# A two-layer decoder on one core: GpSimd takes over the last splits, xr_apply and an earlier rstd, and the small work of the last attention stands at other heads

## The chip, the cores and the metric

The kernel runs on one core of a Trainium2 chip. The metric is the device time of one execution in microseconds (us); lower is better. Three runs of the kernel before gave 401.40, 405.24 and 403.68 us, median 403.68. One further execution was profiled: 400.37 us.

## What is computed

Eight sequences (B = 8) of 256 positions (S = 256) with 128 features (D = 128) go through six residual steps. All attention inputs come from a layer norm.

```python
x = x + _L0_attn_ref(_layernorm(x), ...)               # 16 heads, head size 8
x = x + _L0_xattn_ref(_layernorm(x), ctx_1024, ...)    # one head of 128, CROSS
x = x + _L0_ffn_ref(_layernorm(x), ...)                # routed, 2 x 256 rows
x = x + _L1_attn_ref(_layernorm(x), ...)               # one head, causal, CAUSAL
x = x + _L1_xattn_ref(_layernorm(x), ctx_1024, ctx_1024, ...)  # 16 heads, LAST
x = x + _L1_ffn_ref(_layernorm(x), ...)                # light FFN for all rows,
# heavy FFN for the 128 rows of each sequence that a coordinate descent selects

att = softmax(einsum('bhqd,bhkd->bhqk', q, k) / sqrt(head size))
out = einsum('bhqk,bhkd->bhqd', att, v)
```

The heavy rows of the last step are chosen by scores s = x . routing_token, followed by 50 steps of coordinate descent over the 256 positions and a top-128.

## The kernel before

Each of the five engines runs a program that is written out by hand: the order of the work on an engine is the order of the calls in its function, and engines wait for each other on semaphores. An engine takes its instructions strictly in order, so what stands behind a waiting instruction waits too.

The span has four stages. The first attention (16 heads) lies at about 10 to 125 us; the middle, with items of CROSS, CAUSAL and the first few of LAST and the routed FFN, to about 228 us; the last attention (16 heads, keys and values from the context) to 347 us; then the tail with ranks, coordinate descent and the two FFNs. The work items are numbered in `WORK`: 0 to 7 the first attention, 8 to 26 the middle, 27 to 31 the rest of LAST. The eight LAST items are 18, 22, 26, 27, 28, 29, 30, 31; as steps of a 16-head attention they are also counted m = 8 to 15 (`item(m)` and `many(n)` translate), and the sequences are taken in this order as b = 0 to 7.

The last attention runs iterations i = 8 to 15, each over heads h = 0 to 15. Iteration i does, on TensorE, the scores of m = i again (with the maximum subtracted, s_ps, L1321) and the first scores of m = i + 1 (L1330), whose maximum per row VectorE takes (`row_max`, L938, from PSUM); ScalarE makes the exponentials (L643), and TensorE sums the values (`weighted_sum`, L1367) once in four heads. Around these stand the small steps of other items:

- For the item three steps ahead, x: `ln_stats` (VectorE, L911 and L914), `rstd_step_` (GpSimd, L503 and L505), `ln_apply` (VectorE, L922), `xn_transpose` (TensorE, L1269), `xnT_copy` (ScalarE), `qk_project` (L1277, L1281), `qk_copy` (ScalarE, L665, writes qkf), and `split`. `split` takes the fp32 queries and keys in qkf apart into three bf16 terms with four instructions (L399, L401, L402, L404). The sync queue (SP) then writes the terms into the stack that the score matmuls read, in twelve transfers (L462). `v_project` and `v_copy` make the values at h = 14 and 15.
- For i - 1: `normalise` (VectorE), `o_transpose` and `out_project` (TensorE, L1398), `residual` (VectorE, L957).
- For i - 2: `z_norm_stats` and `z_route` (VectorE, L1023 to L1037: moments of the row, and its product with the routing vector), `z_norms` (GpSimd, L551 to L566), `xr_apply` (VectorE, L1045: centred and scaled rows for the last FFN), `xr_transpose` (TensorE, L1392).

prep_ps, one place in PSUM, serves several of TensorE's small steps in turn: `prep_free` holds what the next one has to wait for. qkf has two slots, an item n uses n % 2, so that `qk_copy(n)` waits for the readers of item n - 2. Splits of m = 8, 9 and 10 are on VectorE (at items 18 and 22 of the middle and at h = 6 of iteration 8), those of m = 11 to 15 on GpSimd. GpSimd's program for these is the loop

```python
elif 2 <= n < B or n >= B + AHEAD_C:
    rstd_step_(item(n))
add_bias(n)
if lo == B and n >= lo + 5:
    z_norms(n - lo - 5)
if lo == B and n == lo + 5:
    heavy_bias_parts()
if n not in FIRST:
    split(pool, n)
```

`add_bias` (L513) and `value_bias` (L519) add a bias to x ahead of its residual; `heavy_bias_parts` is seven small instructions of the last FFN, needed in the tail. `f_norm_stats`, `f_rstd_step`, `f_apply` (L1007) are the layer norm of the routed FFN; `softmax_bias` (L966 to L979) is VectorE's part of a CAUSAL item. The functions that the change touches and those that call them:

## Time and profile before

| | us | share of the span |
|---|---|---|
| median of three runs | 403.68 | |
| profiled execution | 400.37 | |
| its span | 398.6 | |
| TensorE matmuls (PE) | 355.0 | 89% |
| TensorE weight loads (PEld) | 210.8 | 53% |
| VectorE (DVE) | 324.3 | 81% |
| ScalarE (ACT) | 265.1 | 67% |
| GpSimd (POOL) | 140.8 | 35% |

The mean granted TensorE clock of this execution was 0.983 of full speed. Weight loads overlap matmuls. A line of the page such as "L938 DVE TENSOR_REDUCE negmax_sb<-s_ps 128x2 bf16<-128x512 f32 x256" is a group of 256 instructions of line 938 of the kernel, with output and input and their shapes. A bracket behind a row, as [1.20 <-DVE negmax_sb L938], is time in which the engine stood idle before it, and the instruction that released it. A row with x2 or more joins neighbouring instructions of a line, and its time is from the first start to the last end. The chain of work that ended last consists of 55% TensorE, 22% VectorE, 6% ScalarE, 5% GpSimd and 3% transfers.

### The profile page before, as it was taken

The page shows a single profiled execution, that of the slowest core. Times are in us where ns is not written, and L with a number is a line of the kernel's source. Part 1 is how long each engine was busy: PE and PEld are TensorE (multiplying, and loading weights), DVE is VectorE, ACT ScalarE, POOL GpSimd, SP SyncE. Part 2 cuts the span into 40 slices and gives each one's busy share as a digit, 9 for nine tenths or more (in the row PEclk, how much of TensorE's full clock was granted, in tenths as well). Part 3 has the DMA queues.
Part 4 walks back from the last instruction along what each step waited for, and adds up shares of the span by engine and source line. Part 5 has one row for each costly group of instructions (what it writes and reads, how often), then busy time and mean ns, then how long its engine had stood idle before and what let it go on. Part 6 is the DMA issues. An engine that isn't in the chain of part 4 may idle for free.

```text
span 398.6 us, 9595 instructions
## 1 busy us (share of the span) xinstructions
PE 355.0 (89%) x3246; PEld 210.8 (53%) x3246; DVE 324.3 (81%) x898; ACT 265.1 (67%) x594; POOL 140.8 (35%) x243
## 2 busy tenths in 40 slices
PE   6999999999999889977797867999889899989994
PEld 5775454545444478866286633444344344447664
DVE  6778989998996377895569585899999997579995
ACT  3446888888878567755507755778767787765751
POOL 8633754475100033342004323447555221280001
PEclk9999999999999999996999997899999999999999
DMA  7442332223420000002000203220321200000003
GB/s 221 126 106 67 82 103 75 72 51 102 130 86 2 2 0 3 0 16 66 0 2 21 62 2 102 59 62 22 82 61 28 75 2 4 2 0 2 0 2 105
DMA packets 35829, 19.99 MB, mean 50 GB/s; under 512 B 4150, under 2 KB 34790, under 8 KB 35782
## 3 DMA queue, kind: packets, MB, share of 16 engines
q1 hardware_dynamic: 34982, 17.81, 16.8%
q10 hardware_dynamic: 608, 1.18, 0.8%
q8 instruction: 27, 0.44, 0.5%
q0 software_dynamic: 192, 0.39, 0.4%
q14 instruction: 20, 0.16, 0.1%
HBM read 5.58 MB, written 1.05 MB: 17 GB/s over the span
## 4 chain that ended last, share of the span: by engine, by line
PE 55%; DVE 22%; issue 7%; ACT 6%; POOL 5%; DMA 3%; SPq 2%; ACTq 0%; POOLq 0%; DVEq 0%
PE pv_ps L1367 11%; PE s_ps L1321 10%; DVE negmax_sb L938 8%; PE s_ps L1424 4%; PE out_ps L1479 3%; PE s_ps L1447 3%; PE s_ps L1655 3%; PE s_ps L1330 3%; PE prep_ps L1277 2%; ACT probT_sb L643 2%; PE s_ps L1507 2%; DVE xn_sb L922 2%; SPq L462 2%; PE out_ps L1398 2%; PE prep_ps L1281 2%
## 5 line engine op out<-in xcount | busy, mean ns | idle before, releaser
L938 DVE TENSOR_REDUCE negmax_sb<-s_ps 128x2 bf16<-128x512 f32 x256 | 163.3, 688 | 25.1 <-PE s_ps L1330 24.8
L643 ACT ACTIVATE probT_sb<-s_ps 128x512 f32<-128x512 f32 x256 | 142.3, 596 | 35.0 <-PE s_ps L1321 32.5
L1321 PE MATMUL s_ps<-stack_sb 63*128 63x256 bf16 x512 | 90.2, 275 | 11.2 <-DVE negmax_sb L938 3.7
L1330 PE MATMUL s_ps<-stack_sb 62*128 62x256 bf16 x512 | 87.3, 275 | 1.9 <-DVE negmax_sb L938 1.4
L1367 PE MATMUL pv_ps<-probT_sb,v_aug_sb 128*32 128x256 f32 x1024 | 69.9, 391 | 0.5 <-ACT probT_sb L643 0.5
L1321 PEld LDWEIGHTS s_ps<-stack_sb 63*128 63x128 bf16 x512 | 31.0, 94 | 68.5 <-ACT probT_sb L643 41.9
L503 POOL TENSOR_SCALAR rstd_sb<-mv_sb 128x2 f32<-128x2 f32 x32 | 7.1, 222 | 118.0 <-DVE mv_sb L914 117.9
L1367 PEld LDWEIGHTS pv_ps<-probT_sb,v_aug_sb 128*32 128x32 f32 x1024 | 27.0, 110 | 25.8 <-issue 13.2
L1330 PEld LDWEIGHTS s_ps<-stack_sb 62*128 62x128 bf16 x512 | 29.6, 94 | 7.3 <-DVE negmax_sb L938 3.2
L665 ACT ACTIVATE qkf_sb<-prep_ps,b_qkv_sb 128x256 f32<-128x256 f32 x56 | 23.9, 470 | 11.9 <-PE prep_ps L1281 10.3
L1189 DVE SCALAR_TENSOR_TENSOR late_sb<-late_sb,level_sb,k_inv_sb 8x256 f32<-8x256 f32 x49 | 23.2, 474 | 1.8
L505 POOL TENSOR_TENSOR rstd_sb<-rstd_sb,minus_half_sb 128x2 f32<-128x2 f32 x32 | 23.1, 722 | 2.7
L922 DVE TENSOR_SCALAR xn_sb<-x_all_sb,mv_sb,rstd_sb 128x128 f32<-128x128 f32 x64 | 20.4, 384 | 3.1 <-POOL rstd_sb L505 2.8
L1277 PE MATMUL prep_ps<-xnT_sb,w_att_sb 128*128 128x256 f32 x64 | 21.5, 418 | 0.3
L1424 PE MATMUL s_ps<-xrT_sb,d_w_sb 128*128 128x512 f32 x40 | 19.5, 611 | 0.8 <-ACT late_sb L730 0.8
L399 POOL CAST parts_sb<-qkf_sb 128x512 bf16<-128x512 f32 x11 | 6.7, 610 | 31.4 <-ACT qkf_sb L665 26.8
L730 ACT ACTIVATE late_sb<-s_ps,d_b_sb 128x512 f32<-128x512 f32 x20 | 13.4, 686 | 6.1 <-PE s_ps L1424 6.1
L513 POOL TENSOR_TENSOR x_all_sb<-x_all_sb,b_vo_sb 128x256 f32<-128x256 f32 x16 | 12.3, 775 | 14.1 <-DVE xn_sb L922 14.1
L991 DVE SCALAR_TENSOR_TENSOR x_all_sb<-out_ps,den_inv_sb,x_all_sb 128x128 f32<-128x128 f32 x32 | 9.7, 346 | 8.4 <-PE out_ps L1479 8.2
L745 ACT ACTIVATE prob_sb<-s_ps,negbias_sb 128x256 f32<-128x256 f32 (+1 forms) x32 | 14.0, 447 | 3.0 <-DVE negbias_sb L979 3.0
L911 DVE BATCH_NORM_STATS2 stats_sb<-x_all_sb 128x6 f32<-128x128 f32 x64 | 15.2, 280 | 0.5 <-DMA x_all_sb<-x 0.3
L1655 PE MATMUL s_ps<-d_w_sb,late_sb 128*128 128x128 f32 x128 | 15.6, 275 | 0.0
(207 smaller groups left out, 647.2 us busy)
## 6 DMA issues: line engine op xcount, KB each, us to landing
stack_sb<-parts_sb SPq DMA_DIRECT2D x186, 64.0 KB, 2.1
x_all_sb<-x SPq DMA_DIRECT2D x4, 256.0 KB, 3.0
ctxT_sb<-ctxT ACTq DMA_DIRECT2D x2, 512.0 KB, 6.3
f_w_sb<-f_w SPq DMA_DIRECT2D x2, 512.0 KB, 3.7
out<-x_all_sb SPq DMA_DIRECT2D x4, 256.0 KB, 2.4
d_w_sb<-d_w SPq DMA_DIRECT2D x2, 320.0 KB, 3.6
w_att_sb<-w_att SPq DMA_DIRECT2D x2, 256.0 KB, 4.0
stack_sb<-maxrow_sb ACTq DMA_DIRECT2D x32, 4.0 KB
```

The source lines that it names most:

```text
L505: pool.tensor_tensor(rstd[:, u, :], rstd[:, u, :], minus_half[:, 0:NT], ALU.pow).then_inc(rstd_ready, 1)
L643: act.activation(probT[:, c % 8], s2_ps[c % 2][:, :, :], ACT.Exp, scale=DH ** -0.5).then_inc(exp_ready, 1)
L665: act.activation(qkf[:, n % 2, a, :], prep_ps[:, a, :], ACT.Identity, bias=b_qkv[:, layer(n), a:a + 1]).then_inc(qk_ready, 2 if layer(n) = ...
L922: i = dve.tensor_scalar(xn[:, u, k, :], x_all[:, tiles(n).start + k, :], mv[:, u, k, 0:1], rstd[:, u, k:k + 1], ALU.subtract, ALU.mult)
L938: dve.tensor_reduce(negmax[:, n % 2, :, max_column(max_head(h))], first_bank(c)[:, :, :], axis=AX.X, op=ALU.max, negate=True).then_inc(max ...
L1189: dve.scalar_tensor_tensor(out=min_junk[:, :], in0=e_row[:, :], scalar=level[:, a:a + 1], in1=k_inv[:, :], op0=ALU.min, op1=ALU.mult, accu ...
L1277: i = pe.matmul(prep_ps[:, 0, :], w_att[:, l, 0, :], xnT[:, u, :], start=True, stop=True)
L1321: i = pe.matmul(s2_ps[c % 2][:, k, :], stack[rows, s3, 1, h // 2, k * P:(k + 1) * P], stack[rows, s3, 0, h // 2, :], start=True, stop=True)
L1330: i = pe.matmul(first_bank(c)[:, k, :], stack[rows, s3, 0, hp, k * P:(k + 1) * P], stack[rows, s3, 1, hp, :], start=True, stop=True)
L1367: i = pe.matmul(pv_ps[0][32 * j:32 * j + 32, g // 2, :], v_cols[:, k, first:first + 32], probT[:, h % 8, k, :], start=(g % 2 == 0 and k == ...
L1424: pe.matmul(up_bank(c), d_w1[:, f, :], xrT[:, 2 * S * q:2 * S * (q + 1)], start=True, stop=True).then_inc(d_h_psum, 1)
L1655: i = pe.matmul(heavy_bank(b)[:, k, :], d_hT[:, q % 2, f, toks[k]], d_w2[:, f, :], start=False, stop=(f == NC - 2 and k == NT - 1))
```

## The change

Three parts. (1) qkf gets a third slot, which the LAST items of the middle (18, 22, 26) use; `before(n)` gives the last item in the same slot, for which `qk_copy(n)` waits. (2) The splits of m = 8, 9 and 10 go from VectorE to GpSimd's loop over the middle, `xr_apply` goes from VectorE to GpSimd for all sequences, and in the last attention GpSimd makes `rstd` one item earlier; `heavy_bias_parts` goes behind the split. (3) In the last attention the small steps stand at other heads: on VectorE ln_stats at h = 11 of the iteration before (was 1), ln_apply 3 (was 2), normalise 5 (4), residual 13 (15), z_norm_stats 1 (3), z_route 8 (7); on ScalarE xnT_copy 5 (3), qk_copy 8 (7), oT_copy 10 (11); on TensorE xn_transpose 5, behind the weighted sum (4, ahead of it), qk_project 8 (7), o_transpose 10 (11), out_project 12 (15).

```diff
-        qkf = sb("qkf", [P, 2, 2, S])
+        qkf = sb("qkf", [P, 3, 2, S])
+        def slot(n):
+            return 2 if WORK[n][0] == LAST and n < MID_END else n % 2
+        def before(n):
+            return max((j for j in range(n) if slot(j) == slot(n)), default=None)
         def split(eng, m):
-            n, u, w = m, m % 2, item(m) % 2
+            n, u, w = m, m % 2, slot(item(m))
-            def xr_late(b):
+            def xr_apply(b):
                 pool.wait_ge(rn_ready, b + 1)
-                pool.wait_ge(xrT_psum, b - 1)
+                if b >= 2:
+                    pool.wait_ge(xrT_psum, b - 1)
                         if layer(n - 2) == CAUSAL:
                             value_bias(n - 2)
+                        if layer(n - 3) == LAST:
+                            split(pool, many(n - 3))
                     value_bias(LAST_ITEM)
+                    split(pool, B + 2)
-                    elif 2 <= n < B or n >= B + AHEAD_C:
+                    elif 2 <= n < B or n == B + AHEAD_C:
                         rstd_step_(item(n))
                     add_bias(n)
                     if lo == B and n >= lo + 5:
                         z_norms(n - lo - 5)
+                    if lo == B and lo + AHEAD_C <= n < lo + B - 1:
+                        rstd_step_(item(n + 1))
+                    if lo == B and n >= lo + 5:
+                        xr_apply(n - lo - 5)
+                    if n not in FIRST:
+                        split(pool, n)
                     if lo == B and n == lo + 5:
                         heavy_bias_parts()
-                    if n not in FIRST:
-                        split(pool, n)
             for b in range(3, B):
                 z_norms(b)
-                if b >= B - 2:
-                    xr_late(b)
+                xr_apply(b)
...
-                if n >= 2:
-                    if IS_MID[n - 2]:
-                        act.wait_ge(sc_psum, mid(n - 2) + 1)
+                j = before(n)
+                if j is not None:
+                    if IS_MID[j]:
+                        act.wait_ge(sc_psum, mid(j) + 1)
...
-                        if layer(i) == LAST and i != MID_END - 1:
-                            split(dve, many(i))
...
+                        if lo == B and h == 11 and prepared(i + 1, lo):
+                            ln_stats(prepared(i + 1, lo))
-                        if h == at(lo, 0, 1) and ln is not None and ln != 1:
+                        if (lo == 0 and h == 0 or (i, h) == (B, 1)) and ln is not None and ln != 1:
-                        if (i, h) == (B, 6):
-                            split(dve, B + 2)
-                        if h == 2 and ln is not None and ln != 1:
+                        if h == at(lo, 2, 3) and ln is not None and ln != 1:
-                        if h == 4 and has(i - 1, lo):
+                        if h == at(lo, 4, 5) and has(i - 1, lo):
-                        if h == 15 and has(i - 1, lo):
+                        if h == at(lo, 15, 13) and has(i - 1, lo):
-                            if h == 3:
+                            if h == 1:
                                 z_norm_stats(i - 2 - B)
-                            if h == 7:
+                            if h == 8:
                                 z_route(i - 2 - B)
-                            if h == 12:
-                                xr_apply(i - 2 - B)
...
+                        if lo == B and h == 5 and x is not None:
+                            if prep_free:
+                                pe.wait_ge(*prep_free)
+                            xn_transpose(x)
+                            prep_free = (xnT_ready, x + 1)
-                        if h == 7 and x is not None:
+                        if h == at(lo, 7, 8) and x is not None:
                             qk_project(x)
-                        if h == 11 and has(i - 1, lo):
+                        if h == at(lo, 11, 10) and has(i - 1, lo):
                             o_transpose(i - 1)
-                        if h == 15 and has(i - 1, lo):
+                        if h == at(lo, 15, 12) and has(i - 1, lo):
                             out_project(i - 1)
```

What the change does to the order of the instructions is shown at three places. The first is GpSimd around the start of the last attention. In the kernel before, value_bias (L519) is followed by three add_bias (L513), rstd of item 27 (L503, L505), the add_bias of m = 11 and the split of m = 11:

```order
L519 TENSOR_TENSOR x_all_sb<-x_all_sb,b_vo_sb 128x256 x2
L513 TENSOR_TENSOR x_all_sb<-x_all_sb,b_vo_sb 128x256 x3
L503 TENSOR_SCALAR rstd_sb<-mv_sb 128x2
L505 TENSOR_TENSOR rstd_sb<-rstd_sb,minus_half_sb 128x2
L513 TENSOR_TENSOR x_all_sb<-x_all_sb,b_vo_sb 128x256
L399 CAST parts_sb<-qkf_sb 128x2x256
```

In the changed kernel lines have shifted by 8: value_bias is L527, split L407 to L412, add_bias L521, rstd L511 and L513:

```order
L527 TENSOR_TENSOR x_all_sb<-x_all_sb,b_vo_sb 128x256 x2
L407 CAST parts_sb<-qkf_sb 128x2x256
L409 TENSOR_TENSOR rest_sb<-qkf_sb,parts_sb 128x512
L410 TENSOR_TENSOR parts_sb<-qkf_sb,parts_sb 128x2x256
L412 TENSOR_TENSOR parts_sb<-rest_sb,parts_sb 128x2x256
L521 TENSOR_TENSOR x_all_sb<-x_all_sb,b_vo_sb 128x256 x3
L511 TENSOR_SCALAR rstd_sb<-mv_sb 128x2
L513 TENSOR_TENSOR rstd_sb<-rstd_sb,minus_half_sb 128x2
L521 TENSOR_TENSOR x_all_sb<-x_all_sb,b_vo_sb 128x256
L511 TENSOR_SCALAR rstd_sb<-mv_sb 128x2
L513 TENSOR_TENSOR rstd_sb<-rstd_sb,minus_half_sb 128x2
L407 CAST parts_sb<-qkf_sb 128x2x256
```

The split of m = 10 has come in between value_bias and the add_bias, ahead of rstd(27), and rstd(28) now stands ahead of the split of m = 11. The second place is GpSimd in the middle, around the routed FFN's rstd (L593 and L595, later L602 and L604). Before:

```order
L593 TENSOR_SCALAR f_rstd_sb<-f_mv_sb 128x4
L595 TENSOR_TENSOR f_rstd_sb<-f_rstd_sb,minus_half_sb 128x4
L519 TENSOR_TENSOR x_all_sb<-x_all_sb,b_vo_sb 128x256
L503 TENSOR_SCALAR rstd_sb<-mv_sb 128x2
L505 TENSOR_TENSOR rstd_sb<-rstd_sb,minus_half_sb 128x2
```

and in the changed kernel:

```order
L602 TENSOR_SCALAR f_rstd_sb<-f_mv_sb 128x4
L604 TENSOR_TENSOR f_rstd_sb<-f_rstd_sb,minus_half_sb 128x4
L527 TENSOR_TENSOR x_all_sb<-x_all_sb,b_vo_sb 128x256
L407 CAST parts_sb<-qkf_sb 128x2x256
L409 TENSOR_TENSOR rest_sb<-qkf_sb,parts_sb 128x512
L410 TENSOR_TENSOR parts_sb<-qkf_sb,parts_sb 128x2x256
L412 TENSOR_TENSOR parts_sb<-rest_sb,parts_sb 128x2x256
L511 TENSOR_SCALAR rstd_sb<-mv_sb 128x2
```

Here the split of m = 8 has come in behind value_bias(19) and ahead of rstd(22). The third place is GpSimd in iteration 10, where z_norms(0) ends with xr_scale. Before, heavy_bias_parts (prob_sb, the first three of its seven rows) follows, and then the split of m = 13:

```order
L562 TENSOR_SCALAR rnorm_sb<-rnorm_sb 128x2
L564 TENSOR_TENSOR rnorm_sb<-rnorm_sb,minus_half_sb 128x2
L566 TENSOR_TENSOR xr_scale_sb<-rnorm_sb,z_rstd_sb 128x2
L573 MEMSET prob_sb 128x128
L574 MEMSET prob_sb 128x128
L575 CAST prob_sb<-d_b_sb 3x128
```

and in the changed kernel:

```order
L574 TENSOR_TENSOR xr_scale_sb<-rnorm_sb,z_rstd_sb 128x2
L511 TENSOR_SCALAR rstd_sb<-mv_sb 128x2
L513 TENSOR_TENSOR rstd_sb<-rstd_sb,minus_half_sb 128x2
L596 TENSOR_SCALAR xr_sb<-x_all_sb,z_mv_sb,xr_scale_sb 128x128 x2
L407 CAST parts_sb<-qkf_sb 128x2x256
L409 TENSOR_TENSOR rest_sb<-qkf_sb,parts_sb 128x512
L410 TENSOR_TENSOR parts_sb<-qkf_sb,parts_sb 128x2x256
L412 TENSOR_TENSOR parts_sb<-rest_sb,parts_sb 128x2x256
L581 MEMSET prob_sb 128x128
```

Between z_norms and the split there is now rstd of the next item and xr_apply, and heavy_bias_parts has gone behind the split.

## Rows read from the trace of the kernel before

**Rows 1.** Windows, iterations 8 to 13: length, PE, PEld, DVE, ACT, POOL, clock.

```profile
228.06:247.42 19.36, 13.14 (x132) 6.25 (x132) 14.21 (x29) 10.91 (x22) 5.69 (x7) 0.91 0.18 45
247.42:261.86 14.44, 14.44 (x152) 7.04 (x153) 11.98 (x24) 10.96 (x24) 5.72 (x7) 0.88 0.21 52
261.86:276.37 14.51, 13.63 (x156) 6.67 (x156) 14.36 (x37) 11.56 (x26) 7.87 (x21) 1.00 0.23 58
276.37:291.45 15.08, 13.66 (x155) 6.58 (x156) 13.94 (x33) 11.40 (x25) 10.26 (x18) 1.00 0.22 54
291.45:306.74 15.29, 13.81 (x155) 6.59 (x155) 15.17 (x36) 11.51 (x25) 8.30 (x16) 1.00 0.21 54
306.74:319.48 12.74, 11.50 (x145) 5.32 (x145) 12.67 (x31) 10.11 (x21) 2.98 (x9) 1.00 0.25 64
```

**Rows 2.** Waits of 262 to 333 us: engine, line, releaser: total, times, longest.

```profile
PE prep_ps L1269 <- DVE xn_sb L922: 2.2, 3, 0.9
...
PE s_ps L1321 <- DVE negmax_sb L938: 2.1, 5, 0.8
```

**Rows 3.** Instructions of xr_apply: on VectorE in two stretches, on GpSimd.

```profile
L1045 DVE TENSOR_SCALAR xr_sb<-x_all_sb,z_mv_sb,xr_scale_sb x4: 1121/1162/1202, 288.4 to 304.7; 128x128 f32<-128x128 f32 x4
...
L1045 DVE TENSOR_SCALAR xr_sb<-x_all_sb,z_mv_sb,xr_scale_sb x6: 333/336/342, 317.7 to 344.4; 128x128 f32<-128x128 f32 x6
...
L587 POOL TENSOR_SCALAR xr_sb<-x_all_sb,z_mv_sb,xr_scale_sb x4: 792/798/811, 351.9 to 357.9; 128x128 f32<-128x128 f32 x4
```

**Rows 4.** Timeline of VectorE, then of GpSimd, iteration 11.

```profile
288.39 2.25 DVE L1045 TENSOR_SCALAR xr_sb<-x_all_sb,z_mv_sb,xr_scale_sb 128x128 f32<-128x128 f32 x2
...
287.60 0.61 POOL L399 CAST parts_sb<-qkf_sb 128x512 bf16<-128x512 f32 x1
288.29 1.16 POOL L401 TENSOR_TENSOR rest_sb<-qkf_sb,parts_sb 128x512 f32<-128x512 f32 x1
...
290.64 1.16 POOL L404 TENSOR_TENSOR parts_sb<-rest_sb,parts_sb 128x512 bf16<-128x512 f32 x1
```

**Rows 5.** Timeline of TensorE at the end of iteration 11.

```profile
290.05 0.71 PE L1398 MATMUL out_ps<-w_att_sb,oT_sb 128*128 128x128 f32 x4
291.08 0.44 PE L1392 MATMUL prep_ps<-ident_sb,xr_sb 128*128 128x128 f32 x2 [0.32 <-ACT v_aug_sb L699]
```

**Rows 6.** Iteration 8: chain of waits, timelines of TensorE, ScalarE, GpSimd.

```profile
235.57 0.43 DVE parts_sb L399
...
238.07 0.53 SPq L462
...
245.11 2.06 DMA stack_sb<-parts_sb
...
238.92 0.27 PE L1321 MATMUL s_ps<-stack_sb 63*128 63x256 bf16 x1 [1.20 <-DVE negmax_sb L938]
...
247.42 0.27 PE L1321 MATMUL s_ps<-stack_sb 63*128 63x256 bf16 x1 [2.49 <-DMA stack_sb<-parts_sb]
...
225.83 0.84 ACT L665 ACTIVATE qkf_sb<-prep_ps,b_qkv_sb 128x256 f32<-128x256 f32 x2 [0.67 <-PE prep_ps L1281]
...
231.34 0.71 POOL L505 TENSOR_TENSOR rstd_sb<-rstd_sb,minus_half_sb 128x2 f32<-128x2 f32 x1
232.83 0.72 POOL L513 TENSOR_TENSOR x_all_sb<-x_all_sb,b_vo_sb 128x256 f32<-128x256 f32 x1 [0.78 <-DVE xn_sb L922]
```

**Rows 7.** Busy time by window, iteration 9; last columns clock, DMA, GB/s.

```profile
248.20:251.60 3.40, 3.40 (x29) 1.57 (x22) 2.76 (x10) 2.48 (x6) 0.95 (x2) 0.51 0.39 101
```

**Rows 8.** Middle, item 18: timelines of GpSimd, VectorE, TensorE.

```profile
175.38 1.05 POOL L519 TENSOR_TENSOR x_all_sb<-x_all_sb,b_vo_sb 128x256 f32<-128x256 f32 x1
...
178.48 1.08 DVE L1007 TENSOR_SCALAR f_xn_sb<-x_all_sb,f_mv_sb,f_rstd_sb 128x128 f32<-128x128 f32 x4
...
180.81 0.60 DVE L922 TENSOR_SCALAR xn_sb<-x_all_sb,mv_sb,rstd_sb 128x128 f32<-128x128 f32 x2
...
181.56 0.66 PE L1269 MATMUL pv_ps<-ident_sb,xn_sb 128*128 128x128 f32 x2 [4.37 <-DVE xn_sb L922]
```

20 lines of the change are left out of this document (6 added, 14 removed).

## Prediction

> **What bounds the kernel now.** I read the page first: TensorE is busy 89% of the span, VectorE 81%, ScalarE 67% and GpSimd 35%. TensorE comes first, but the share is a mean over stages, so I cut the last attention at the first score matmul of each iteration (the table of windows, [rows 1]). Iteration 8 takes 19.36 us and TensorE works 13.14 of them. Iteration 9 takes 14.44, all of it TensorE, at a granted clock of 0.88. Iterations 10, 11 and 12 take 14.51, 15.08 and 15.29, with 13.6 to 13.8 us of TensorE and 14.36, 13.94 and 15.17 of VectorE. In 13, and 14 is like it, VectorE is busy 12.67 of 12.74 us: there VectorE is the bound. The table of waits says what TensorE stands for in 10 to 14: xn (2.2 us) and the row maxima (2.1 us), both VectorE's [rows 2]. So work taken from VectorE pays in iteration 8 and in 10 to 14, and only down to TensorE's own work, 13.6 to 13.8 us and its small gaps in 10 to 12.
>
> **What goes from VectorE in 10 to 14: xr_apply.** Its row is the key to the change. Alone, one of its two instructions takes 336 ns; in iterations 11 and 12 it takes 1121 to 1202 [rows 3]. The timelines say why: at 288.39 VectorE starts the pair and needs 2.25 us, while GpSimd's split has a 1.16 us operation at 288.29, a second behind it, and its last at 290.64 [rows 4]. The pair ends as the second does: each of the two waited for one GpSimd instruction. On GpSimd xr_apply takes 2 x 0.80 us [rows 3].
> The Trainium skill (SBUF — State Buffer, "Who interferes with whom") says that a VectorE tensor_scalar in a two-port mode and a GpSimd instruction take a shared pair of ports for a whole instruction each, and that tensor_reduce never contends; this trace agrees (1162 ns against 336). Were the ports shared by halves, the pair would have taken some 1.2 us, and its removal 1 us less in 11 and 12.
>
> VectorE so gets back some 0.5 us (the pair overlapped, alone) in 10, 13 and 14 and 2.2 in 11 and 12. Most of TensorE's wait for xn goes too: ln_stats moves to h=11 of the iteration before, and xn_transpose stands a head later, behind a weighted_sum. Against this, out_project (0.71 us at 290.05) now stands at h=12. At h=15 it filled time in which TensorE waits for v_copy anyway; 0.32 us of that wait are left before xr_transpose [rows 5], and it grows by what out_project covered. So I do not take TensorE's 13.7 us as the new period of 10, 11 and 12 but 14.0: -0.5, -1.1 and -1.3. For 13 and 14 I take -0.6 and -0.4, for 15, which has little of this, -0.1. **Sum of 10 to 15: -4.0.**
>
> **Iteration 8.** The chain of waits [rows 6] runs from VectorE's split(10) (235.57 to 238.06) through the sync queue's twelve issues (238.07 to 245.11) to the last transfer's 2.06 us and TensorE's wait of 2.49 us at 247.42: 9.1 us from the split's end. TensorE also waited 1.20 us at 238.92 (and twice 0.20 behind it) for row maxima queued behind the split. The first excerpt shows split(10) on GpSimd ahead of the last attention. What it needs is qk_copy(26), at 225.83 and over by 226.7, in the new third slot. At 0.61 and three times 1.16, 4.2 with its gaps [rows 4], it ends near 231.0, its transfers land near 240.1, and both waits, 4.1 us, go. But rstd(27) then stands behind the split and three add_bias of 0.72: 231.0 + 2.2 + 0.95 = 234.1, against 232.05 now. ln_apply(27) follows, xn_transpose comes at about 234.85, and TensorE stands up to 1.8 us there, partly in place of 0.8 that it stood before. It would reach iteration 9 between 243.0 and 244.7, the second if half the clock is granted again near its end, as the iteration's mean of 0.91 shows it now. I take 243.9: **-3.5** (-2.7 to -4.4).
>
> **Iteration 9.** From 248.2 to 251.6 the granted clock is 0.51, the 1.2 GHz level, with TensorE busy throughout [rows 7]; just before, it had stood for 2.49 us. Half the speed for 3.4 us is 1.7 us lost. Without the standing most of it should go: **-1.5** (0 to -1.7). The price is read; that the standing is its cause, one trace can't show.
>
> **The middle, item 18.** VectorE's split(8) goes to GpSimd, which can start it only behind value_bias(19) (175.38, 0.7 us without company) and ends it near 180.4 (second excerpt). In that time VectorE, earlier than now by a split of some 2.5 us, comes to f_apply's four tensor_scalars, of xr_apply's kind, which alone take 1.08 us together [rows 8]. If each waits for one GpSimd operation, as xr_apply's did, they run after 176.1, 176.8, 177.9 and 179.1, and the small product behind them near 180.3. Then come softmax_bias, 1.3, and ln_apply(21) near 181.6, against 180.8: +0.8. The other end is no collision: 2.5 us early. TensorE waits for exactly this xn, 4.37 us up to 181.56 [rows 8]. I take the nearer row, the collision: **+0.8** (-2.5 to +0.9). At item 22 VectorE's split is followed by a wait for TensorE: 0.
>
> **Sum.** -4.0 - 3.5 - 1.5 + 0.8 = -8.2 us. The profiled execution took 400.37 us (span 398.6 and 1.8 around it), so 392.2 is what I expect of its like. It lies 3.3 below the median of the runs, 403.68; against that I say 395.5. The tail's three further xr_apply, 3 x 1.6 us, fall to an engine that idles there: 0; if they were on the path, +1. One per cent, 4 us, is about what a measurement of this kernel can tell from no change.
>
> **Rivals.**
> A. *TensorE keeps most of it (within 1%).* Iteration 9 is all TensorE already, and 10 to 12 stand only 0.9 to 1.5 us above its busy time. If out_project at h=12 and the moved transposes put their 0.7 us on the path and the half clock comes anyway, 10 to 12 give 0.8 and not 2.9, iteration 9 nothing, iteration 8 its lower end 2.7, 13 to 15 their 1.1; less 0.8 in the middle that is 3.8: **399.9**. For it speaks iteration 9; against it TensorE's waits for VectorE in 10 to 14.
>
> B. *GpSimd becomes the bound (slower).* Its order in 11 is z_norms, rstd, xr_apply, split (third excerpt). Now the split starts 11.2 us into iteration 11 (287.60 less 276.37); rstd and xr_apply ahead of it add 2.55, z_route a head later some 0.3, and the split is 4.2: it ends 18.3 in, or 4.3 into iteration 12. With 9.1 to the last landing that is 13.4 of 14.0 us. split(15), without an rstd, ends some 3 us into 13: 12.1 of 12.1, no margin. Each microsecond by which GpSimd comes later beyond about 0.3 costs one in 11, 12 and 13. The gain is gone from 3 us on (3 x 2.7 = 8.1); at 4.5 us it is 3 x 4.2 - 8.2 = +4.4, **408**. For it speaks that GpSimd's busy time rises from 7.9 to 10.3 us by 1.6 in each of 10 to 12; against it, that this still leaves over 2 us of 14 and that what it waits for comes earlier.
> The Trainium skill (GPSIMD Engine Reference, "Performance versus the Vector engine") has GpSimd at 1.96 times VectorE's time for elementwise work and VectorE as the rule. The rows say more, 0.80 to 0.34 for xr_apply. By the rule the moves should lose; they do only in rival B.
>
> C. *The middle gains as well (faster).* f_apply slips in before GpSimd's split, ln_apply(21) comes 2.5 us early, and TensorE's shorter wait spares a half clock behind it as in iteration 9, 1.7 us: -8.2 - 0.8 - 2.5 - 1.7 = -13.2, **390.5**. For it speaks the length of that wait; against it, that value_bias holds f_apply until 176.1 already.
>
> **Chances.** The forecast has 0.50, with a range of its own of 392.5 to 398.5; C 0.16; A 0.24; B 0.10. So faster by over 1% is 0.66, within 1% 0.24, slower 0.10. The range, 390 to 401, leaves out B and the far halves of A and C.
>
> **What would show it.** Right are: an iteration 9 that begins without a wait for a transfer and at full clock; iterations 10 to 12 near 14.0 us with VectorE below 13, and 13 and 14 near 12.1; GpSimd's rstd(27) 2 us late in iteration 8; f_apply's four at about 1.1 us each. Rival A is seen as TensorE busy for the whole of 10 to 12 at 14.5; rival B as waits of TensorE for stack transfers or xr at the ends of 11 to 13. I am wrong in kind if half clock shows in more places than now, or if VectorE is still full in 11 and 12.

## The result, and the profile after

The changed kernel takes 399.93 us (median of 20 runs, 398.02 to 403.75) where the kernel before takes 404.35 (20 runs, 401.40 to 406.21). The ratio is 0.992, 95% interval 0.990 to 0.994: it is faster by 0.8%, some 3.3 us (the two medians alone are 4.4 apart), and not by the 8.2 us of the forecast. The ratios in this document are not quotients of medians, and executions over 1.5% above the fastest of the same kernel are left out of them. A second measurement of both, beside the experiments, gave 0.993 (0.989 to 0.996). By the bound of 1% this is the outcome "within 1%", and the 399.9 us lie where rival A had put them, though only in part for rival A's reasons, as will be seen. The profiled execution of the changed kernel took 402.32 us, over its own median, where that of the kernel before, 400.37, lay 4 us under its own. So the two pages differ the wrong way round, and the readings below go by stages.

The page of the changed kernel: the span, the busy times, and the chain by engine.

```profile
span 400.5 us, 9589 instructions
...
PE 355.7 (89%) x3246; PEld 212.1 (53%) x3246; DVE 314.8 (79%) x874; ACT 266.9 (67%) x594; POOL 160.4 (40%) x267
...
PE 69%; DVE 9%; ACT 8%; issue 6%; POOL 5%; DMA 1%; ACTq 0%; POOLq 0%; DVEq 0%
```

VectorE has lost 9.5 us and GpSimd gained 19.6. The chain that ended last was 55% TensorE and 22% VectorE; it is 69% and 9% now. VectorE has indeed been taken off the path. Below are the windows of iterations 8 to 14, with the columns of [rows 1]; here and from now on each iteration is cut at its first exponential on ScalarE. Lines have moved: L1324 and L1333 are the scores, L1395 is xr_transpose, L1023 f_apply, L954 row_max.

```profile
232.75:249.93 17.18, 13.22 (x132) 6.04 (x134) 12.45 (x30) 10.61 (x23) 9.16 (x14) 0.90 0.19 47
249.93:264.00 14.07, 13.09 (x154) 6.53 (x153) 12.17 (x26) 11.46 (x25) 6.14 (x8) 1.00 0.23 59
264.00:279.04 15.04, 13.57 (x158) 6.75 (x156) 13.20 (x33) 11.57 (x25) 9.24 (x18) 1.00 0.22 55
279.04:293.98 14.94, 13.47 (x158) 6.65 (x154) 13.53 (x33) 11.75 (x25) 11.58 (x25) 1.00 0.22 55
293.98:308.92 14.94, 13.47 (x158) 6.65 (x154) 12.81 (x29) 11.75 (x25) 10.08 (x17) 1.00 0.22 55
308.92:321.19 12.27, 11.36 (x148) 5.22 (x144) 11.98 (x27) 10.21 (x21) 5.32 (x11) 1.00 0.27 66
321.19:333.45 12.26, 11.37 (x144) 5.22 (x140) 11.98 (x29) 10.22 (x21) 4.24 (x10) 1.00 0.01 3
```

Against [rows 1]: iteration 8 is 2.2 us shorter, 9 is 0.4 shorter at full clock, 10 is 0.5 longer, 11 and 12 are 0.1 and 0.3 shorter. VectorE has 1.4 to 2.1 us to spare in 10 to 12, TensorE's busy time is as before, and it idles 1.5 us in each. 13 and 14 are 0.5 and 0.1 shorter. Iteration 15 took 14.73 us before and takes 15.61 now.

The table has the lengths of the stages in two profiles of each kernel (the second ones are from the experiments). "Middle" runs from the first exponential of iteration 7, in the first attention, to that of iteration 8. Each star marks 3.4 us at half clock.

| stage | before | before, second | after | after, second | forecast of the difference |
|---|---|---|---|---|---|
| middle | 104.50 ** | 103.76 * | 106.89 *** | 106.85 *** | +0.8 |
| iteration 8 | 19.33 * | 20.52 * | 17.18 * | 17.17 * | -3.5 |
| 9 | 14.46 * | 15.23 ** | 14.07 | 14.07 | -1.5 |
| 10, 11, 12 | 44.87 | 44.93 | 44.92 | 44.92 | -2.9 |
| 13, 14 | 25.13 | 25.15 | 24.53 | 24.50 | -1.0 |
| 15 | 14.73 | 14.73 | 15.61 | 15.63 | -0.1 |

(In the second profile of the kernel before, the 6.8 us counted to iteration 9 begin 1.7 us ahead of it. Iteration 15 ends with its last exponential.) The terms that missed by the most are 10 to 12, by 2.9 us, the middle, by 1.6 and 2.3, and 15, by 1.0. For 10 to 12 and 15 the forecast had -3.0 together, and the measured sum is +0.9. The rows of the table add up to +0.2 us in the first pair of profiles and -1.2 in the second, where the spans differ by +1.9 and +0.4. The rest, 1.9 and 1.7 us, lies ahead of the middle, where the change leaves the order as it was. In the second pair the changed kernel has 3.4 us at half clock there, from 21.0 us; in the first neither kernel has, and the cause is open.

### The profile page after: what moved, and what is told of

Same layout as the page of the kernel before. It is cut to its first block, busy times and chain, and to the rows that moved or that the text cites. A ratio compares the mean times of both kernels' runs of the same rounds, so it can differ in the third digit from the quotient of the medians.

```text
span 400.5 us, 9589 instructions
## 1 busy us (share of the span) xinstructions
PE 355.7 (89%) x3246; PEld 212.1 (53%) x3246; DVE 314.8 (79%) x874; ACT 266.9 (67%) x594; POOL 160.4 (40%) x267
## 4 chain that ended last, share of the span: by engine, by line
PE 69%; DVE 9%; ACT 8%; issue 6%; POOL 5%; DMA 1%; ACTq 0%; POOLq 0%; DVEq 0%
PE pv_ps L1370 15%; PE s_ps L1324 14%; PE s_ps L1427 4%; PE prep_ps L1280 3%; PE s_ps L1450 3%; ACT probT_sb L658 3%; PE s_ps L1333 3%; PE out_ps L1482 3%; PE s_ps L1663 3%; PE prep_ps L1284 2%; PE out_ps L1401 2%; PE s_ps L1510 2%; DVE negmax_sb L954 2%; PE s_ps L1467 2%; PE prep_ps L1307 2%
## 5 line engine op out<-in xcount | busy, mean ns | idle before, releaser
L954 DVE TENSOR_REDUCE negmax_sb<-s_ps 128x2 bf16<-128x512 f32 x256 | 163.9, 690 | 30.9 <-PE s_ps L1333 30.5
L658 ACT ACTIVATE probT_sb<-s_ps 128x512 f32<-128x512 f32 x256 | 144.3, 595 | 32.6 <-PE s_ps L1324 28.3
L1324 PE MATMUL s_ps<-stack_sb 63*128 63x256 bf16 x512 | 89.4, 273 | 9.2 <-ACT probT_sb L658 5.1
L1333 PE MATMUL s_ps<-stack_sb 62*128 62x256 bf16 x512 | 85.9, 274 | 3.8 <-DMA stack_sb<-parts_sb 2.4
L1324 PEld LDWEIGHTS s_ps<-stack_sb 63*128 63x128 bf16 x512 | 31.1, 94 | 64.4 <-ACT probT_sb L658 34.0
L511 POOL TENSOR_SCALAR rstd_sb<-mv_sb 128x2 f32<-128x2 f32 x32 | 7.1, 223 | 106.1 <-DVE mv_sb L930 105.9
L1333 PEld LDWEIGHTS s_ps<-stack_sb 62*128 62x128 bf16 x512 | 29.8, 94 | 9.2 <-DVE negmax_sb L954 3.2
L938 DVE TENSOR_SCALAR xn_sb<-x_all_sb,mv_sb,rstd_sb 128x128 f32<-128x128 f32 x64 | 22.4, 441 | 3.9 <-POOL rstd_sb L513 3.6
L513 POOL TENSOR_TENSOR rstd_sb<-rstd_sb,minus_half_sb 128x2 f32<-128x2 f32 x32 | 22.9, 714 | 2.7
L407 POOL CAST parts_sb<-qkf_sb 128x512 bf16<-128x512 f32 x14 | 8.5, 609 | 28.9 <-ACT qkf_sb L681 28.9
L521 POOL TENSOR_TENSOR x_all_sb<-x_all_sb,b_vo_sb 128x256 f32<-128x256 f32 x16 | 11.5, 726 | 16.0 <-DVE xn_sb L938 15.9
L412 POOL TENSOR_TENSOR parts_sb<-rest_sb,parts_sb 128x512 bf16<-128x512 f32 x14 | 16.2, 1158 | 1.1
L409 POOL TENSOR_TENSOR rest_sb<-qkf_sb,parts_sb 128x512 f32<-128x512 f32 x14 | 16.2, 1156 | 1.1
```

The source lines that it names most:

```text
L409: eng.tensor_tensor(rest[:, :, :], qkf[:, w], parts[:, u, :, 0, :], ALU.subtract).then_inc(rest_ready, 1)
L513: pool.tensor_tensor(rstd[:, u, :], rstd[:, u, :], minus_half[:, 0:NT], ALU.pow).then_inc(rstd_ready, 1)
L658: act.activation(probT[:, c % 8], s2_ps[c % 2][:, :, :], ACT.Exp, scale=DH ** -0.5).then_inc(exp_ready, 1)
L938: i = dve.tensor_scalar(xn[:, u, k, :], x_all[:, tiles(n).start + k, :], mv[:, u, k, 0:1], rstd[:, u, k:k + 1], ALU.subtract, ALU.mult)
L954: dve.tensor_reduce(negmax[:, n % 2, :, max_column(max_head(h))], first_bank(c)[:, :, :], axis=AX.X, op=ALU.max, negate=True).then_inc(max ...
L1324: i = pe.matmul(s2_ps[c % 2][:, k, :], stack[rows, s3, 1, h // 2, k * P:(k + 1) * P], stack[rows, s3, 0, h // 2, :], start=True, stop=True)
```

## The experiments

All times are compared with runs of the kernel before on the same chip. "Middle" and the iterations are cut as above.

### 1. GpSimd's moves alone, and the heads alone

e1_moves keeps the splits of m = 8, 9 and 10 and xr_apply on GpSimd and puts all the rest back:

```diff
-                        if lo == B and h == 11 and prepared(i + 1, lo):
-                            ln_stats(prepared(i + 1, lo))
-                        if (lo == 0 and h == 0 or (i, h) == (B, 1)) and ...
+                        if h == at(lo, 0, 1) and ln is not None and ln != 1:
-                    if lo == B and lo + AHEAD_C <= n < lo + B - 1:
-                        rstd_step_(item(n + 1))
...
-                        if h == at(lo, 15, 12) and has(i - 1, lo):
+                        if h == 15 and has(i - 1, lo):
                             out_project(i - 1)
```

> The changed kernel with the small steps of the last attention at the heads of the kernel before, and rstd not one item earlier: what is left is GpSimd's splits of m = 8, 9, 10 and xr_apply. Theory H (the moved heads took the saving back: in the changed kernel TensorE waits 0.96 us for v_copy at the end of each of iterations 10 to 12, where out_project stood, and 0.5 us behind the moved xn_transpose): iterations 10 to 12 fall from 14.95 to 14.2-14.5 us, iteration 8 stays at 17.2, and the time is 397 to 398.5 us, ratio to before 0.983 to 0.987. Rival M (the moves to GpSimd gain only what iteration 8 shows, the heads are neutral or help): iterations 10 to 12 at 14.9 or more, time 400 or more, ratio 0.990 or above.

Measured: 404.87 us, ratio 1.002 (0.999 to 1.005): no gain. Yet iterations 9, 10 and 12 are 13.35, 14.52 and 14.52 us, up to 0.7 shorter than in the changed kernel. What eats the gain stands in its windows of iterations 10 and 11,

```profile
266.36:280.88 14.52, 13.62 (x158) 6.67 (x154) 13.34 (x34) 11.23 (x24) 8.32 (x16) 1.00 0.22 57
280.88:298.99 18.11, 15.01 (x158) 7.13 (x154) 13.61 (x33) 11.40 (x26) 12.57 (x26) 0.91 0.18 45
```

and in its timeline of GpSimd in iteration 11,

```profile
284.26 0.41 POOL L589 TENSOR_TENSOR prob_sb<-prob_sb 3x128 bf16<-3x128 f32 x1
...
285.08 0.73 POOL L513 TENSOR_TENSOR rstd_sb<-rstd_sb,minus_half_sb 128x2 f32<-128x2 f32 x1
```

and of TensorE:

```profile
286.59 0.41 PE L1268 MATMUL prep_ps<-ident_sb,xn_sb 128*128 128x128 f32 x2 [2.78 <-DVE xn_sb L936]
```

rstd waits on GpSimd until split and the last part of heavy_bias_parts (L589) are through, xn is 2.78 us late, and half clock follows (3.4 us from 287.1): 3.6 us in one iteration. In iteration 8 the same wait is 2.81 us long and 6.8 us at half clock begin in it. This is the mechanism of rival B, in the two places where rstd is queued behind a split. Theory H had the time wrong (397 to 398.5 us) and was right about the iterations that have no such wait. Rival M's "400 or more" holds, but not its 14.9 us or more for them.

e2_heads is the other half: everything on VectorE as before, the small steps at the heads of the change, rstd one item earlier.

```diff
-        qkf = sb("qkf", [P, 3, 2, S])
+        qkf = sb("qkf", [P, 2, 2, S])
-            return 2 if WORK[n][0] == LAST and n < MID_END else n % 2
+            return n % 2
-                        if layer(n - 3) == LAST:
-                            split(pool, many(n - 3))
...
+                            if h == 12:
+                                xr_apply(i - 2 - B)
```

> The kernel before with only the small steps of the last attention at the heads of the changed kernel, and GpSimd's rstd one item earlier; splits and xr_apply stay on VectorE. Theory H: iteration 8 as before (19.3 us), iterations 11 and 12 at 15.3 or above, since v_copy's wait of 0.96 us and the stretched xr_apply are both there; time 405 to 407 us, ratio 1.002 to 1.007. Rival M: iterations 10 to 12 shorter by 0.3 to 0.5 us since xn comes in time; ratio 0.995 to 0.998.

Measured: 403.82 us, ratio 1.002 (0.998 to 1.005). Iterations 10 to 12 take 15.04, 15.07 and 15.15, and 15 takes 15.75; neither theory's ratio (1.002 to 1.007, 0.995 to 0.998) can be told apart from this one. In 10 this is to the hundredth the changed kernel's 15.04, with the same two waits of TensorE, 0.51 and 0.96 us, though nothing has gone to GpSimd: it is the heads that set this length. The start of iteration 9 on TensorE shows the wait for the stack, here longer than in [rows 6]:

```profile
250.25 0.27 PE L1335 MATMUL s_ps<-stack_sb 63*128 63x256 bf16 x1 [4.04 <-DMA stack_sb<-parts_sb]
```

So neither half gains anything alone, and together they give 0.8%. What joins them is rstd and ln_stats: the moves need them earlier, as e5 shows for iteration 11.

### 2. out_project back at h = 15

e3_out15 is the changed kernel but for this:

```diff
-                        if h == at(lo, 15, 12) and has(i - 1, lo):
+                        if h == 15 and has(i - 1, lo):
                             out_project(i - 1)
-                        if h == at(lo, 15, 13) and has(i - 1, lo):
+                        if h == 15 and has(i - 1, lo):
                             residual(i - 1)
```

> The changed kernel with out_project and residual alone back at h = 15. Theory H: TensorE's wait for v_copy falls from 0.96 to 0.32 us and iterations 9 to 12 lose 0.6 us each, 10 to 12 at 14.3; time 397 to 398 us, ratio 0.983 to 0.985. Rival: the 0.6 us show up again as a wait for the row maxima or for the exponentials (iterations 10 to 12 stay at 14.9), ratio 0.991 to 0.993.

Measured: 399.04 us, ratio 0.990 (0.984 to 0.995), not told apart from the changed kernel. TensorE's timeline in iteration 10:

```profile
271.24 0.28 PE L1324 MATMUL s_ps<-stack_sb 63*128 63x256 bf16 x1 [0.47 <-ACT probT_sb L658]
...
274.88 0.44 PE L1395 MATMUL prep_ps<-ident_sb,xr_sb 128*128 128x128 f32 x2 [0.32 <-ACT v_aug_sb L715]
```

The wait for v_copy fell from 0.96 to 0.32 us, as theory H had it, but a wait of 0.47 for the exponentials came up behind o_transpose and oT_copy at h = 10, and the iterations are 14.83 instead of 14.94. 0.6 us fell to 0.1: the rival was nearer. One step put back does not undo the set.

### 3. The split of m = 8 back on VectorE

```diff
-                        if layer(n - 3) == LAST:
+                        if layer(n - 3) == LAST and n - 3 != LAST_AT[0]:
                             split(pool, many(n - 3))
...
+                        if i == LAST_AT[0]:
+                            split(dve, many(i))
```

> The changed kernel with the split of m = 8 alone back on VectorE at item 18. Theory C (collision): f_apply's four instructions fall from 4.28 to about 1.1 us, TensorE's wait for xn(21) from 5.25 to 4.4 us, and the middle is 0.9 us shorter; time 399.0 us, ratio 0.987 to 0.990. Rival: VectorE's own split of 2.9 us stands in its place and more, the wait stays at 5 us or more, ratio 0.992 or above.

Measured: 399.66 us, ratio 0.990 (0.986 to 0.993). First what the changed kernel shows at item 18, on GpSimd,

```profile
176.96 0.73 POOL L527 TENSOR_TENSOR x_all_sb<-x_all_sb,b_vo_sb 128x256 f32<-128x256 f32 x1
177.64 0.61 POOL L407 CAST parts_sb<-qkf_sb 128x512 bf16<-128x512 f32 x1
...
180.68 1.15 POOL L412 TENSOR_TENSOR parts_sb<-rest_sb,parts_sb 128x512 bf16<-128x512 f32 x1
```

on VectorE,

```profile
177.62 4.28 DVE L1023 TENSOR_SCALAR f_xn_sb<-x_all_sb,f_mv_sb,f_rstd_sb 128x128 f32<-128x128 f32 x4
```

and on TensorE:

```profile
184.31 0.66 PE L1272 MATMUL pv_ps<-ident_sb,xn_sb 128*128 128x128 f32 x2 [5.25 <-DVE xn_sb L938]
```

The four instructions of f_apply take 4.28 us where they took 1.08 [rows 8]: from the start of the split to 181.9, the end of its last operation. With the split back on VectorE, e4's rows of VectorE and of TensorE are those of the kernel before:

```profile
183.20 1.08 DVE L1023 TENSOR_SCALAR f_xn_sb<-x_all_sb,f_mv_sb,f_rstd_sb 128x128 f32<-128x128 f32 x4
```

```profile
186.28 0.66 PE L1274 MATMUL pv_ps<-ident_sb,xn_sb 128*128 128x128 f32 x2 [4.36 <-DVE xn_sb L938]
...
233.56 0.27 PE L1326 MATMUL s_ps<-stack_sb 63*128 63x256 bf16 x1 [0.99 <-DMA stack_sb<-parts_sb]
```

The wait goes from 5.25 to 4.36 us: the collision costs TensorE 0.89 us. The middle is 105.25 us, 1.6 less than in the changed kernel, but with 6.8 us at half clock where that has 10.2. The last row is of the start of iteration 8, and it was not in the forecast: a wait of 0.99 us for the transfers of stack, which e3 has too (0.93). The split of m = 9 ends at 221.5 in the changed kernel, where VectorE had it done by 215.4 in the kernel before. In the changed kernel's own profile the wait is hidden: TensorE is slower there by 3.4 us at half clock from 217.6, in which it is busy throughout:

```profile
217.60:221.00 3.40, 3.40 (x15) 3.13 (x14) 0.58 (x3) 1.21 (x3) 3.24 (x4) 0.50 0.00 1
```

e4 also has an iteration 8 in the changed kernel's order at full clock. It takes 14.64 us, and TensorE, which began it 1.0 us later against GpSimd's work, waits 0.46 us for xn where it waits 1.22 in the changed kernel (shown in section 4):

```profile
233.97:248.61 14.64, 11.61 (x132) 5.62 (x134) 12.44 (x30) 10.59 (x21) 8.15 (x13) 1.00 0.22 56
```

### 4. The small steps back, but ln_stats and rstd early

e5_stats11 is e1_moves with ln_stats at h = 11 of the iteration before and rstd one item earlier:

```diff
+                        if lo == B and h == 11 and prepared(i + 1, lo):
+                            ln_stats(prepared(i + 1, lo))
+                    if lo == B and lo + AHEAD_C <= n < lo + B - 1:
+                        rstd_step_(item(n + 1))
```

> The changed kernel with all small steps of the last attention at the heads of the kernel before, but ln_stats at h = 11 of the iteration before and GpSimd's rstd one item earlier, as in the change. Theory Q (what undid e1_moves is rstd queued on GpSimd behind split and heavy_bias_parts: 2.78 us of wait for xn in iteration 11 and half clock after it): iteration 11 falls from 18.1 to 14.5 us, 9 stays at 13.35, 10 and 12 at 14.5; iterations 9 to 15 are 3 us shorter than in the changed kernel; time 396.5 to 397.5 us, ratio 0.980 to 0.984. Rival: the gain of the change needs its heads, and the ratio stays at 0.990 or above.

The changed kernel itself ran beside it, as e0_after, for a second profile.

> The changed kernel unaltered, for a second profile of it beside its variants. Both theories on the clock agree on iterations 9 to 15 (14.1, 15.0, 14.9, 14.9, 12.3, 12.3, 15.6 us at full clock) and on TensorE's 5.25 us wait at item 19 of the middle. Theory K (the half clock follows TensorE's long waits): the stretch at half clock in the middle, after that wait, is there again, and iteration 8 has one only where a wait of over 1 us stands in it. Rival: the stretches lie elsewhere, without a wait before them. Ratio to before 0.990 to 0.994.

Measured: the changed kernel 401.98 us, ratio 0.993; e5_stats11 401.47 us, ratio 0.990 (0.983 to 0.997), where 0.980 to 0.984 was expected. Iteration 11 fell from 18.1 to 14.58, 9 is 13.35, 10 is 14.13, 12 is 14.56 and 15 is 14.72; 9 to 15 are 2.5 us shorter than in the changed kernel. In time this is hardly seen, since iteration 8 now is 18.61, with TensorE's wait of 2.81 us and 6.8 us at half clock behind its start.

e6_split89 puts the splits of m = 8 and 9 back on VectorE as well:

```diff
-                        if layer(n - 3) == LAST:
-                            split(pool, many(n - 3))
+                        if layer(i) == LAST and i != MID_END - 1:
+                            split(dve, many(i))
```

> e5_stats11 with the splits of m = 8 and 9 back on VectorE (items 18 and 22). Theory: TensorE's wait for xn(21) is 4.4 us and not 5.25, its wait of about 0.95 us for the transfers of stack at the start of iteration 8 is gone, the middle is 1 to 2 us shorter; time 395 to 396 us, ratio 0.976 to 0.980. Rival: the middle's length is set elsewhere, no change against e5_stats11.

Measured: 399.62 us, ratio 0.990 (0.987 to 0.993). The middle fell from 107.13 to 104.40 us, more than the expected 1 to 2 us and with 3.4 us less at half clock, but the time did not follow to the expected 395 to 396; iteration 8 is 19.04 with the same wait.

e7_rstd27 moves rstd(27) on GpSimd:

```diff
                     split(pool, B + 2)
+                    rstd_step_(item(B + AHEAD_C))
                 for n in range(lo, lo + B):
...
-                    elif 2 <= n < B or n == B + AHEAD_C:
+                    elif 2 <= n < B:
                         rstd_step_(item(n))
```

> e6_split89 with rstd(27) ahead of the three add_bias on GpSimd. Theory: TensorE's wait for xn in iteration 8 loses up to 2 us (from 2.8 to about 0.8) and the half clock that lay in that iteration goes; iteration 8 at 14.0 to 14.6 us; time 393.5 to 395 us, ratio 0.973 to 0.977. Rival: the wait only moves to the next step and the time is that of e6_split89.

Why it stands to be moved is seen in the changed kernel's GpSimd in iteration 8,

```profile
234.03 1.16 POOL L412 TENSOR_TENSOR parts_sb<-rest_sb,parts_sb 128x512 bf16<-128x512 f32 x1
235.26 2.10 POOL L521 TENSOR_TENSOR x_all_sb<-x_all_sb,b_vo_sb 128x256 f32<-128x256 f32 x3
...
237.63 0.72 POOL L513 TENSOR_TENSOR rstd_sb<-rstd_sb,minus_half_sb 128x2 f32<-128x2 f32 x1
```

and its TensorE:

```profile
239.14 0.41 PE L1272 MATMUL prep_ps<-ident_sb,xn_sb 128*128 128x128 f32 x2 [1.22 <-DVE xn_sb L938]
```

The last operation of split(10) ends at 235.2, the three add_bias take 2.10 us, rstd(27) is done at 238.35 and xn_transpose waits 1.22. Split(10) itself began at 231.0, when qk_copy(26) was through; in this all is as forecast. Measured: 396.78 us, ratio 0.983 (0.978 to 0.988). That is above the expected 393.5 to 395. Iteration 8 is 16.67, with 3.4 us at half clock, where 14.0 to 14.6 was expected; of the wait 1.67 us are left, not 0.8:

```profile
238.81 0.41 PE L1273 MATMUL prep_ps<-ident_sb,xn_sb 128*128 128x128 f32 x2 [1.67 <-DVE xn_sb L937]
```

### 5. One head later, in iteration 8 and everywhere

e8_item8 is e7_rstd27 with item 27's steps in iteration 8 at the heads of the change:

```diff
-                        if h == 4 and x is not None:
+                        if h == 4 and x is not None and i != B:
...
+                        if (i, h) == (B, 5) and x is not None:
+                            if prep_free:
+                                pe.wait_ge(*prep_free)
+                            xn_transpose(x)
```

> e7_rstd27 with the steps of item 27 in iteration 8 alone one head later (ln_apply 3, xn_transpose 5 behind the weighted sum, xnT_copy 5, qk 8, as in the change). Theory: TensorE's wait for xn in iteration 8 falls from 1.67 us to under 0.5, iteration 8 from 16.67 to 14.5 to 15.0 us at full clock, and no half clock stands in it; time 1 to 2 us under e7_rstd27, 395 us, ratio 0.976 to 0.980. Rival: 0.5 us of wait for the exponentials takes its place and the gain is under 1 us.

Measured: 395.63 us, ratio 0.975 (0.971 to 0.979). This is the fastest of the orders without work of no use: 2.5% under the kernel before. The window of its iteration 8:

```profile
228.13:242.69 14.56, 11.70 (x132) 5.72 (x134) 12.78 (x30) 10.61 (x23) 9.17 (x14) 1.00 0.22 55
```

14.56 us at full clock, against 17.18 and 19.33. The wait for xn is gone, one of 0.47 us for the exponentials is there.

e9_xn5 does so in all iterations (`lo == B` in place of `i == B`), and e10_out12 takes e7_rstd27 and puts out_project at h = 12 and residual at 13:

```diff
-                        if h == 15 and has(i - 1, lo):
+                        if h == (12 if lo else 15) and has(i - 1, lo):
                             out_project(i - 1)
```

> e7_rstd27 with those steps one head later in all iterations of the last attention. Theory: in iterations 9 to 14 TensorE's wait of 0.46 us for xn goes and one of 0.51 us for the exponentials comes in its place; iterations 9 and 10 get 0.3 to 0.5 us longer (13.35 to 13.7, 14.13 to 14.5), 11 and 12 stay within 0.1 of 14.6; against e8_item8 the time is 1 us more. Rival: later is better everywhere, 11 and 12 fall to 14.1.

> e7_rstd27 with out_project at h = 12 and residual at h = 13, as in the change. Theory: TensorE's wait for v_copy at the end of iterations 10 to 12 is 0.96 us and not 0.32, and 9 to 12 are each 0.6 us longer (10: 14.7, 11 and 12: 15.2); 2.5 us in all, ratio 0.988 to 0.990. Rival: only the place of the idle time changes, as in e3_out15, where the wait fell but 14.94 became 14.83: under 0.2 us each.

Measured: e9_xn5 397.27 us, ratio 0.982 (0.978 to 0.985); e10_out12 403.97 us, ratio 0.999 (0.996 to 1.002), where 0.988 to 0.990 was expected. By stages:

| iteration | 9 | 10 | 11 | 12 | 13 | 14 | 15 |
|---|---|---|---|---|---|---|---|
| changed kernel | 14.07 | 15.04 | 14.94 | 14.94 | 12.27 | 12.26 | 15.61 |
| e7_rstd27 | 13.35 | 14.14 | 14.60 | 14.58 | 12.97 | 12.36 | 14.73 |
| e8_item8 | 13.35 | 14.13 | 14.60 | 14.58 | 12.34 | 12.34 | 14.73 |
| e9_xn5 | 13.80 | 14.80 | 14.80 | 14.80 | 12.35 | 12.35 | 14.73 |
| e10_out12 | 14.30 | 15.27 | 15.23 | 15.17 | 13.08 | 13.36 | 15.89 |

One TensorE row of e9 says where the later xn_transpose is paid: a wait of 0.85 us behind it, for the row maxima and not for the exponentials as the theory had it. Iteration 10 is 0.67 us longer than in e8, 11 and 12 are 0.2 longer.

```profile
279.12 0.27 PE L1325 MATMUL s_ps<-stack_sb 63*128 63x256 bf16 x1 [0.85 <-DVE negmax_sb L953]
```

Two rows of e10 say what out_project at h = 12 costs:

```profile
273.13 0.71 PE L1402 MATMUL out_ps<-w_att_sb,oT_sb 128*128 128x128 f32 x4 [0.50 <-ACT oT_sb L751]
...
277.42 0.44 PE L1396 MATMUL prep_ps<-ident_sb,xr_sb 128*128 128x128 f32 x2 [0.96 <-ACT v_aug_sb L714]
```

It waits 0.50 us for oT_copy, and v_copy's wait at the end is 0.96. Iterations 11 and 12 are 15.2 us as expected, 10 is 15.27 and not 14.7, and 14 and 15, for which nothing was expected, are 1.0 and 1.2 longer than in e7. With xn_transpose and o_transpose moved as well, the 0.50 goes, and the changed kernel's iteration 11 has these:

```profile
284.75 0.27 PE L1324 MATMUL s_ps<-stack_sb 63*128 63x256 bf16 x1 [0.51 <-ACT probT_sb L658]
...
293.19 0.44 PE L1395 MATMUL prep_ps<-ident_sb,xr_sb 128*128 128x128 f32 x2 [0.96 <-ACT v_aug_sb L715]
```

### 6. Filling TensorE's wait in the middle

The profiles of the kernels up to e7 have 10 to 24 us at half clock ahead of the tail. To see whether TensorE's standing brings it, e11_fill puts matmuls that do nothing into the wait for xn(21):

```diff
                             pe.wait_ge(xnT_ready, n)
+                            if i == FFN_STEP - 1:
+                                stay_busy(30)
                             xn_transpose(n)
```

> e7_rstd27 with thirty matmuls of no use (identity by identity, into the bank that xn_transpose overwrites) put into TensorE's wait for xn(21) in the middle, 4.4 us long; they take some 3.6 us at full clock. Theory K (the standing brings the half clock): the stretch of 6.8 us at half clock that begins in this wait is gone, and the middle is 1 to 3 us shorter (104.5 to 102-103.5). Rival: the half clock is there as before, the matmuls run through it and make the middle up to 2 us longer.

Measured: 399.71 us, ratio 0.986 (0.982 to 0.989). TensorE's timeline (each of the thirty shows as two records) and the windows over the fill and over iteration 8:

```profile
180.80 6.86 PE L1267 MATMUL pv_ps<-ident_sb 128*128 128x128 f32 x60
187.50 0.38 PE L1274 MATMUL pv_ps<-ident_sb,xn_sb 128*128 128x128 f32 x2
```

```profile
180.80:187.60 6.80, 6.80 (x63) 6.80 (x62) 4.86 (x23) 1.78 (x7) 3.29 (x6) 1.00 0.35 88
...
236.60:243.40 6.80, 6.17 (x38) 2.77 (x40) 3.69 (x6) 2.54 (x6) 1.77 (x3) 0.50 0.36 90
```

The fill took 6.86 us, not 3.6, and made xn_transpose 2.2 us later than in e7, both counted from the first exponential of iteration 7. Still the middle is 104.22 us, 0.3 shorter than e7's: the half clock in it, 6.8 us in e7, is gone, and cost some 2.5 us. Theory K holds for this place: in all fourteen profiles without a fill half clock begins in this wait or within 0.8 us behind it, and in neither with one. The time did not gain. The fill was too long, and iteration 8 has 6.8 us at half clock here, 3.4 in e7.

> e8_item8 with eighteen matmuls of no use in TensorE's wait for xn(21), where e11_fill had thirty, which took 6.86 us of a wait of 4.4. Eighteen take 4.1. Theory K: no half clock in the middle, xn_transpose on time, the middle at 102 to 103 us where e8_item8 had 103.6 with 3.4 us at half clock; time 1 to 2 us under e8_item8, ratio 0.970 to 0.973. Rival: the half clock only moves to the next standing of TensorE (1.8 us at item 22 or iteration 8), the ratio stays at 0.975 or more.

e12_fill18 is e8_item8 with `stay_busy(18)` at the same place. Its TensorE and the window over the fill:

```profile
180.47 4.18 PE L1267 MATMUL pv_ps<-ident_sb 128*128 128x128 f32 x36
184.91 0.44 PE L1274 MATMUL pv_ps<-ident_sb,xn_sb 128*128 128x128 f32 x2 [0.26 <-DVE xn_sb L938]
```

```profile
180.40:187.20 6.80, 6.54 (x55) 6.20 (x54) 6.01 (x28) 2.96 (x10) 3.21 (x6) 1.00 0.35 88
```

Measured: 394.05 us, ratio 0.974 (0.971 to 0.978); one of the six executions took 1759.6 us, for a reason that is not known. The clock stays full and the middle is 102.02 us, against 103.61 in e8_item8 with 3.4 us at half clock. Half clock does not come up elsewhere between the first attention and the tail, as the rival had it. In the times the two can't be told apart (0.974 and 0.975).

> The kernel before unaltered, for a second profile of it. If the iterations of the last attention are a matter of the order, 10 to 14 come out as before (14.5, 15.1, 15.3, 12.7, 12.4); iteration 8 takes 18.8 to 19.3 us and iteration 9 13.3 without half clock or 14.5 with it. If the two kernels differ by the clock alone, the half clock lies in other places than in the first profile and the periods at full clock are those of the changed kernel. Ratio 1.

The second profile of the kernel before: 404.05 us, ratio 1.000. Iterations 10 to 15 repeat to 0.03 us. Iterations 8 and 9 do not: 35.75 us, against 33.79 in the profile on which the forecast was built. TensorE's row at the start of iteration 9, and the window of the half clock that begins in its wait:

```profile
249.27 0.37 PE L1321 MATMUL s_ps<-stack_sb 63*128 63x256 bf16 x1 [4.05 <-DMA stack_sb<-parts_sb]
```

```profile
248.20:255.00 6.80, 5.73 (x43) 2.52 (x43) 3.69 (x10) 2.92 (x6) 1.67 (x3) 0.50 0.41 106
```

The wait for the stack is 4.05 us here and 2.49 there [rows 6]. The chain from VectorE's split through the twelve issues is as long in both. But the first 3.4 us at half clock lie at 234.6 here, ahead of the split, which begins 8.0 us into the iteration and not 7.1; and TensorE, at full clock from 238.0, comes to the wait 0.6 us earlier.

## Why the prediction was wrong

**The direction and three terms held.** Both waits that the chain of iteration 8 had shown are gone, split(10) began and ended as worked out from its neighbours, rstd(27) came late for the reason given (counted from iteration 8's first exponential, split(10) ended and rstd(27) was done within 0.1 us of the forecast), and the middle's collision cost 0.88 us where 0.8 was put: the 1.1 us of f_apply became 4.28, each instruction held by one of GpSimd's. This last was the step in which a row of another place (L1045) was carried to f_apply, and the Trainium skill's rule on the shared ports (SBUF — State Buffer, "Who interferes with whom") says the same; the trace agrees (4.28 us against 1.08).

**The step that failed is "I take 14.0 us for 10, 11 and 12".** The sum there took TensorE's 13.7 us and a gap of 0.3. The prediction had itself said that v_copy's wait "grows by what out_project covered", and then did not add it: it is 0.96 us, not 0.3. And it had no term at all for the exponentials: with a weighted sum and xn_transpose ahead of the next scores, ScalarE runs out, and TensorE then waits 0.51 us for it. 13.47 + 0.96 + 0.51 = 14.94, to the hundredth the length of 11 and 12. Both waits stand in iterations 10 and 12 of every profile with all the new heads (the changed kernel twice, e2, e4), and the 0.51 in none of e1 and e5 to e8. The first omission alone does not explain the miss: when e3 took 0.64 us of v_copy's wait away, 0.47 came up for the exponentials behind o_transpose, and 14.94 became only 14.83. The later xn_transpose, which the forecast counted as a gain, costs 0.2 to 0.7 us in each of 9 to 12 by itself (e9 against e8). The heads of before leave 14.13, 14.60 and 14.58 (e8), which would have made this term -1.6. Even that is short of -2.9: 0.44 to 0.47 us of wait for xn and 0.32 for v_copy stay in 11 and 12.

**Iteration 15** was put at -0.1 and is +0.9. It is out_project's place too: 15.89 in e10 against 14.73 in e7, where only it and residual differ, and 15.01 in e3 against 15.61 in the changed kernel.

**Iteration 8** was put at -3.5; it is -2.2 in the first pair of profiles and -3.4 in the second. Of the kernel after both show 17.2, 1.4 more than the 15.8 forecast, with 3.4 us at half clock that the forecast had inside its range only. At full clock the same order takes 14.64 (e4), so that of the 17.2 some 1.8 us are half clock and 0.8 the longer wait for xn behind rstd(27). With rstd(27) ahead of the add_bias it is 14.56 (e8).

**Iteration 9** was put at -1.5. The mechanism was right, it runs at full clock now, but the size was not: the half clock cost 14.46 - 13.35 = 1.1 us (13.35 is TensorE's order of before at full clock, in e1 and e5 to e8), not 1.7: TensorE is busy 13.12 us there, only 1.3 less, and waits 0.23 for ScalarE's maxrow, a wait that was not there before. And of the 1.1 the new heads took 0.7 back (14.07), with waits of 0.51 and 0.47 us for the exponentials.

**The middle** is the second step that failed: item 22 stood in the sum at 0, because VectorE waits behind its split there, and what the later end of that split does to its reader was not asked. It is not 0: GpSimd's split of m = 9 makes TensorE wait 0.9 to 1.0 us at the start of iteration 8, or, where that is hidden, it stands beside 3.4 us of half clock at 217.6, and the middle is 2.4 to 3.1 us longer than before. What brought the half clock at 217.6, with only the 1.8 us wait for ScalarE shortly before it, which the kernel before has too, is open: it is in both profiles of the changed kernel and in e1 and e5, and not in e3, e4 and e6.

**Against the rivals.** A gave the right number, 399.9, from a cause that was half right: not TensorE's busy time is the floor, its waits for ScalarE's v_copy and exponentials are. That it is right to the tenth is luck: A had -0.8 for 10 to 12 and -1.1 for 13 to 15, which came out at 0.0 and +0.3, and it counts from a median of 403.68 that with twenty runs is 404.35. In 9 to 12 VectorE is no longer what TensorE waits for. B's mechanism is real but does not decide: it shows in e1, which is not faster for it, and in iteration 8; the change avoids most of it by taking rstd one item ahead. At the ends of 13 and 14, which B had without margin, TensorE waits some 0.35 us for GpSimd's xr. C did not come.

**How much is the clock?** The granted clock of every timed run is on record. The span times (1 - clock), the time that half clock takes away at most, has a median of 6.0 and 8.0 us in the two series of the changed kernel and of 7.6 to 8.8 in the series of the kernel before. The span less this is 392.7 and 392.3 against 394.2 to 394.7. So of some 3.3 us about two are the order of the work and one is clock, as far as such a division goes. The best order divides likewise: in e8's series the two are 3.5 and 389.8 us, against 8.5 and 394.7 in its series of the kernel before, half and half. And from e6 to e8 nearly all is clock: 8.2, 5.3 and 3.5 us of it in e6, e7 and e8, and 390.2, 389.5 and 389.8 of rest. It explains too why a profile is a poor base for a few microseconds: that of the kernel before lay under all its twenty timed runs. The forecast added 3.3 us to it to stand against the median, and did not ask which stage they came from. By the second profile, with a span 2.9 us longer, 2.0 us are in iterations 8 and 9, 1.6 ahead of the middle, and the middle is 0.7 shorter.

## What to carry to other kernels

When the bounding engine has been freed, the next bound need not be its neighbour's busy time, and here it was not; add up that engine's waits in an iteration in the new order, one by one, above all those that a moved step had been filling. A step that is moved pays or costs by what stands in the gap it leaves: out_project at the end of the iteration cost next to nothing, because TensorE waited there anyway, and at h = 12 it made six of seven iterations 0.6 to 1.2 us longer (e10 against e7). The price depends on the company: in the changed kernel, putting it back gained 0.1 us in each of 10 to 12 and 0.6 in 15 (e3). Where work is moved onto an in-order queue, put the short instruction that others wait for ahead of the long ones; rstd(27) ahead of 2.1 us of add_bias, and its item's steps one head later in that iteration alone, took the ratio from 0.990 to 0.975, more than the whole change did. By the division above most of that came by way of the clock, since the waits that they shortened had half clock beginning in them or just behind.

## What was not expected of the hardware

- Where TensorE stands for some microseconds, the granted clock often falls to 0.50, the 1.2 GHz level, and stays there when the work resumes: beginning in waits of 2.8, 4.05, 4.4 and 5.3 us, for 3.4 or 6.8 us. Matmuls of no use in such a wait kept it at 1.00 (e11, e12), and the middle was 1.6 us shorter with them in e12 than in e8. Standing is not all. Half clock also began at 217.6, where TensorE had been busy for 1.0 us behind a wait of 1.8. And at the start of iteration 8 one profile with a wait of 0.93 us for the stack had 6.8 us at half clock, from 1.1 us behind it (e3), another with 0.99 had none (e4).
- The time of one kernel varied by over 5 us with the clock that it was granted: the changed kernel took 398.0 us at a mean clock of 0.995 and 403.7 at 0.976, in one series.
- A VectorE tensor_scalar that needs 0.27 us (f_apply, 1.08 for four) is held for as long as the GpSimd instruction that runs, 1.15 us, again and again: four took 4.28 us. The row maxima, which VectorE reads from PSUM, kept their 0.6 us beside the same splits.
